# Values of the second layer made for 128 tokens and for four images' compressed rows at a time

## The reference, cut to what matters

```python
v = heads(x @ wv.T)                                      # values of the 64 tokens
windows = x[:, idx, :]                                   # 15 windows of 8 tokens
x_c = einsum('bwrd,r->bwd', windows, softmax(gate_logits))
k_c = x_c @ wk_c.T                                       # keys of the 15 compressed rows
v_c = x_c @ wv_c.T                                       # values of the 15 compressed rows
all_scores = concatenate([comp_scores, win_scores, sink], axis=-1)
attn = softmax(all_scores)
out = einsum('bhqk,bhkd->bhqd', w_comp, v_c) + einsum('bhqk,bhkd->bhqd', w_win, v)
```

## Time and profile before

| | us |
|---|---|
| median of three runs | 2063.84 |
| lowest and highest | 2058.97, 2075.73 |
| the profiled execution | 2071.78 |
| its span, first to last instruction | 2070.0 |

### The profile page before, as it was taken

One profiled execution on the slowest core, in us unless ns is written; L12 is line 12 of the kernel. 1 busy time (PEld: TensorE's weight loads), 2 busy tenths in 40 slices (PEclk: granted clock), 3 DMA queues, 4 the chain that ended last, 5 costly groups with the idle time before them and its releaser, 6 DMA issues.

```text
span 2070.0 us, 47437 instructions
## 1 busy us (share of the span) xinstructions
PE 1745.7 (84%) x15216; PEld 1352.3 (65%) x15216; DVE 1268.4 (61%) x3484; ACT 948.9 (46%) x2291; POOL 950.9 (46%) x770
## 2 busy tenths in 40 slices
PE   1454879989897989899897989899897989998956
PEld 1443766868676776768676776768675776866644
DVE  2566456757675766767575766767675756753432
ACT  0122534546463645456363635445463635553522
POOL 1224245454556555464456464464445554533222
PEclk9999988989999999999898989999998989999986
DMA  6647454544544444545445444544445444301000
GB/s 245 243 163 255 179 201 167 194 154 152 203 183 168 181 168 175 199 148 192 157 178 204 181 155 155 211 158 172 165 168 209 179 136 170 131 20 50 17 26 6
DMA packets 109170, 332.08 MB, mean 160 GB/s; under 512 B 13662, under 2 KB 87585, under 8 KB 92412
## 3 DMA queue, kind: packets, MB, share of 16 engines
q1 hardware_dynamic: 86416, 300.90, 39.5%
q0 software_dynamic: 8992, 19.42, 2.9%
q10 hardware_dynamic: 13516, 8.51, 1.4%
HBM read 299.48 MB, written 29.29 MB: 159 GB/s over the span
## 4 chain that ended last, share of the span: by engine, by line
PE 65%; POOL 10%; issue 9%; DMA 7%; DVE 4%; ACT 2%; ACTq 1%; SPq 1%; POOLq 0%; DVEq 0%
PE hid_bank L598 11%; PE pool_bank L452 6%; DMA outs_d<-ys 5%; PE pool_bank L457 5%; POOL yg L1357 5%; PE sec_bank L654 4%; PE hid_bank L583 4%; PE sec_bank L674 4%; PE hid_bank L582 3%; PE sec_bank L665 3%; POOL xbuf L1346 3%; PE hid_bank L584 2%; PE sec_bank L617 2%; PE sec_bank L634 2%; PE down_bank L543 2%
## 5 line engine op out<-in xcount | busy, mean ns | idle before, releaser
L1346 POOL TENSOR_TENSOR xbuf<-xbuf 128x512 f32<-128x512 f32 x256 | 330.1, 1289 | 528.3 <-DVE xbuf L1039 518.5
L850 ACT ACTIVATE hid<-hid_bank,bias_t 128x128 f32<-128x128 f32 x960 | 273.7, 371 | 122.3 <-PE hid_bank L584 116.4
L598 PE MATMUL hid_bank<-w_s,hid 128*128 x1920 | 291.3, 297 | 0.0
L598 PEld LDWEIGHTS hid_bank<-w_s,hid 128*128 128x128 f32 x1920 | 243.8, 199 | 16.7
L1039 DVE TENSOR_TENSOR xbuf<-xbuf 128x1536 f32<-128x1536 f32 x128 | 236.7, 1849 | 25.9 <-DMA xbuf<-in_x 25.9
L582 PE MATMUL hid_bank<-xt,w_b 128*128 128x128 bf16 x960 | 201.3, 230 | 33.8 <-issue 18.4
L1060 DVE SCALAR_TENSOR_TENSOR taps<-pooled_s,tapw,taps 128x256 f32<-128x256 f32 (+1 forms) x416 | 210.0, 505 | 29.9 <-issue 21.6
L1043 DVE TENSOR_TENSOR xbuf<-xbuf 128x512 bf16<-128x512 f32 x128 | 90.3, 706 | 213.5 <-ACT xbuf L764 213.4
L1384 POOL TENSOR_TENSOR keys_h<-keys,heads 128x632 f32<-128x632 f32 x128 | 198.6, 1578 | 18.1 <-PE sec_bank L654 15.6
L1200 DVE COPY ys<-hid_bank 128x128 f32<-128x128 f32 x240 | 68.8, 287 | 219.0 <-PE hid_bank L598 192.8
L583 PE MATMUL hid_bank<-xt,w_b 128*128 128x128 bf16 x960 | 202.9, 230 | 0.1
(11 more groups left out here) (213 smaller groups left out, 3443.7 us busy)
## 6 DMA issues: line engine op xcount, KB each, us to landing
xbuf<-in_x SPq DMA_DIRECT2D x128, 2048.0 KB
rows_s<-rows_d SPq DMA_DIRECT2D x48, 320.0 KB, 8.9
outs_d<-ys SPq DMA_DIRECT2D x240, 64.0 KB
out<-h ACTq DMA_DIRECT2D x16, 256.0 KB
w_s<-in_w ACTq DMA_DIRECT2D x1, 2560.0 KB
hid<-in_w POOLq DMA_DIRECT2D x10, 256.0 KB, 3.7
rows_d<-x2r,spot_i POOLq DMA_INDIRECT x128
yg<-outs_d,spot_i POOLq DMA_INDIRECT x128
```

The lines of the kernel that those rows point to most:

```text
L598: mm = nc.tensor.matmul(hid_bank[n % 2][:, 0:P], hid[:, n % RING, q * P:(q + 1) * P], w_q, start=False, stop=q == FC - 1)
L850: ins = nc.scalar.activation(hid[:, n % RING, cols], hid_bank[n % 2][:, cols], ACT.Gelu, bias=bias_t[:, q, j:j + 1])
L1346: nc.gpsimd.tensor_tensor(v[:, :, 1, :], v[:, :, 1, :], v[:, :, 2 * k + 3, :], ALU.add) \
```

## The change

`xc` gets 32 columns for each image in place of 15, and is cleared once in the set-up, so that four images' compressed rows are 128 columns. pre.6 makes the values of all tokens of the group, 128 tokens (two images) a product, four products. pre.7 makes the values of the compressed rows, four images a product, two products. ScalarE then moves the result from the partitions on which it came out to each image's: two moves of 64 partitions behind pre.6, four of 15 partitions behind pre.7, where there were two of 79 in all. The lists of all five engines are written anew.

```diff
     sp="""
-        store.9' load.0.0 store.11' load.0.1 store.12' store.10' store.13' store.14' rows.0 rows.1 load.1.0
-        load.1.1 load.2.0 store.0 store.3 load.2.1 store.1 rows.2 store.5 load.3.0 store.2 load.3.1 store.4
-        store.6 store.8 store.7 keep.0""",
+        store.8' store.4' store.6' store.7' load.0.0 store.9' store.12' store.11' store.10' load.0.1 store.13'
+        store.14' rows.0 load.1.0 load.1.1 rows.1 store.2 load.2.0 load.2.1 store.3 rows.2 store.1 store.0
+        store.5 load.3.0 load.3.1 keep.0""",
     pe="""
-        up.0 up.1 table up.2 down.0 up.3 down.1 up.4 up.5 down.2 out' up.6 down.3 down.4 pool.0.0 pool.0.1
-        pool.0.2 up.7 down.5 down.6 att.1 down.7 att.2 lift.0 pool.0.3 lift.1 widen.0 widen.1 lift.2 att.3
-        narrow.0 pre.2 narrow.1 lift.3 widen.2 att.4 pre.3 lift.4 narrow.2 lift.5 pool.1.0 pre.4 pool.1.1 widen.3
-        pre.5 pre.6 pre.7 widen.4 narrow.3 score.0 pool.1.2 score.1 pool.1.3 lift.6 att.7 score.2 score.3 widen.5
-        lift.7 score.4 score.5 narrow.4 score.6 score.7 att.8 widen.6 lift.8 narrow.5 turn.0 widen.7 turn.1
-        lift.9 value.0 pool.2.0 pool.2.1 narrow.6 turn.2 pool.2.2 widen.8 value.1 lift.10 pool.2.3 turn.3 lift.11
...
+        table up.0 up.1 up.2 down.0 up.3 down.1 up.4 down.2 down.3 up.5 out' down.4 pool.0.0 pool.0.1 down.5 up.6
+        pool.0.2 up.7 down.6 att.1 down.7 pool.0.3 lift.0 att.2 lift.1 widen.0 widen.1 att.3 lift.2 narrow.0
+        pre.2 widen.2 pre.3 lift.3 narrow.1 narrow.2 lift.4 pre.4 widen.3 pre.5 lift.5 pre.6 att.4 pool.1.0
+        pool.1.1 pre.7 lift.6 widen.4 narrow.3 score.0 score.1 lift.7 pool.1.2 widen.5 score.2 lift.8 score.3
+        pool.1.3 lift.9 score.4 score.5 narrow.4 att.7 score.6 score.7 lift.10 att.8 narrow.5 widen.6 turn.0
+        lift.11 widen.7 turn.1 value.0 pool.2.0 pool.2.1 narrow.6 turn.2 value.1 widen.8 turn.3 value.2 pool.2.2
...
     act="""
-        hidden.0 table hidden.1 hidden.2 hidden.3 hidden.4 inner.0.0 hidden.5 out' hidden.6 inner.0.1 hidden.7
...
-        inner.1.0 lift.4 gate pre.5 att.6 widen.3 pool.1.0 pre.6 pre.7 lift.5 inner.1.1 pool.1.2 lift.6 widen.4
-        widen.5 pool.1.3 att.7 lift.7 exp inner.2.0 lift.8 turn.0 widen.6 turn.1 pool.2.0 widen.7 inner.2.1
...
+        hidden.0 table hidden.1 hidden.2 hidden.3 inner.0.0 hidden.4 out' hidden.5 inner.0.1 pool.0.0 hidden.6
...
+        inner.1.0 pool.0.3 pre.5 widen.3 lift.5 pre.6 pool.1.0 pre.7 lift.6 widen.4 lift.7 inner.1.1 widen.5
+        lift.8 att.6 gate lift.9 att.7 pool.1.2 exp pool.1.3 lift.10 inner.2.0 turn.0 widen.6 turn.1 inner.2.1
...
-        xc = sb("xc", [C, GI, LC])
+        xc = sb("xc", [C, GI, 2 * LCP])
+        xcw = xc[:, :, 0:LC]
...
-                    half = n - 6
-                    bank = sec_bank[1 - half]
-                    eng.wait_ge(xc_step, at(xc_step, g, 8))
-                    if half == 0:
+                    if n == 6:
                         eng.wait_ge(rope_read, at(rope_read, g, 4))
+                        for t in range(T):
+                            mm = nc.tensor.matmul(b1[:, t * C:(t + 1) * C], x3t[:, t * P:(t + 1) * P], second["v"][:],
+                                                  start=True, stop=True)
                     else:
+                        eng.wait_ge(xc_step, at(xc_step, g, 8))
                         eng.wait_ge(kc_ready, at(kc_ready, g, 1))
-                    for m in range(4):
-                        im = 4 * half + m
-                        nc.tensor.matmul(bank[0:L, m * C:(m + 1) * C], x3t[:, im * L:(im + 1) * L], second["v"][:],
-                                         start=True, stop=True)
-                        mm = nc.tensor.matmul(bank[L:LK, m * C:(m + 1) * C], xc[:, im, :], second["vc"][:],
-                                              start=True, stop=True)
+                        for k in range(2):
+                            mm = nc.tensor.matmul(b0[:, k * C:(k + 1) * C],
+                                                  xc[:, 4 * k:4 * k + 4, :].rearrange("p i w -> p (i w)"), second["vc"][:],
+                                                  start=True, stop=True)
                     mm.then_inc(v_done, 1)
...
-                    half = n - 6
-                    eng.wait_ge(v_done, at(v_done, g, half + 1))
-                    nc.scalar.activation(values[0:LK, 4 * half:4 * half + 4, :, 0:HD].rearrange("p i h d -> p (i h) d"),
-                                         sec_bank[1 - half][0:LK, :].rearrange("p (m d) -> p m d", d=HD), ACT.Copy).then_inc(v_ready, 1)
+                    eng.wait_ge(v_done, at(v_done, g, n - 5))
+                    if n == 6:
+                        if after(g, 1):
+                            eng.wait_ge(o3_done, at(o3_done, g, 0))
+                        for im in range(2):
+                            ins = nc.scalar.activation(values[0:L, im:GI:2, :, 0:HD],
+                                                       b1[im * L:(im + 1) * L].rearrange("p (t h d) -> p t h d", t=T, d=HD),
+                                                       ACT.Copy)
+                    else:
...
+                        for im in range(4):
+                            ins = nc.scalar.activation(values[L:LK, im:GI:4, :, 0:HD],
+                                                       b0[im * 2 * LCP:im * 2 * LCP + LC, 0:2 * C]
+                                                       .rearrange("p (k h d) -> p k h d", k=2, d=HD), ACT.Copy)
+                    ins.then_inc(v_ready, 1)
...
+                nc.gpsimd.memset(xc[:], 0.0).then_inc(ready_p, 1)
                 nc.gpsimd.memset(values[:], 0.0).then_inc(ready_p, 1)
```

More of the change, by code:

```diff
@@ L35 @@
 LK = L + LC
+LCP = 16
 HH = HEADS // 2
@@ L67 @@
-        lift.9 value.0 pool.2.0 pool.2.1 narrow.6 turn.2 pool.2.2 widen.8 value.1 lift.10 pool.2.3 turn.3 lift.11
[L68 to L71, removed]
-    act="""
-        hidden.0 table hidden.1 hidden.2 hidden.3 hidden.4 inner.0.0 hidden.5 out' hidden.6 inner.0.1 hidden.7
-        att.1 pool.0.0 att.2 lift.0 pool.0.2 lift.1 widen.0 widen.1 lift.2 att.3 pre.2 lift.3 pool.0.3 widen.2
-        inner.1.0 lift.4 gate pre.5 att.6 widen.3 pool.1.0 pre.6 pre.7 lift.5 inner.1.1 pool.1.2 lift.6 widen.4
-        widen.5 pool.1.3 att.7 lift.7 exp inner.2.0 lift.8 turn.0 widen.6 turn.1 pool.2.0 widen.7 inner.2.1
[L77 to L80, removed]
@@ L81 @@
-    dve="""
[L82 to L90, removed]
+        table up.0 up.1 up.2 down.0 up.3 down.1 up.4 down.2 down.3 up.5 out' down.4 pool.0.0 pool.0.1 down.5 up.6
@@ new lines @@
+        narrow.7 pool.2.3 att.10 turn.4 lift.12 value.3 widen.9 turn.5 narrow.8 value.4 att.11 turn.6 value.5
+        narrow.9 widen.10 turn.7 value.6 widen.11 value.7 pool.3.0 narrow.10 lift.13 att.12 post.0 widen.12
+        post.1 pool.3.1 narrow.11 lift.14 pool.3.2 narrow.12 widen.13 widen.14 pool.3.3 narrow.13 narrow.14
+        post.3 post.4 post.5""",
+    act="""
+        hidden.0 table hidden.1 hidden.2 hidden.3 inner.0.0 hidden.4 out' hidden.5 inner.0.1 pool.0.0 hidden.6
+        hidden.7 att.1 pool.0.2 lift.0 lift.1 att.2 widen.0 widen.1 lift.2 att.3 pre.2 widen.2 lift.3 lift.4
+        inner.1.0 pool.0.3 pre.5 widen.3 lift.5 pre.6 pool.1.0 pre.7 lift.6 widen.4 lift.7 inner.1.1 widen.5
+        lift.8 att.6 gate lift.9 att.7 pool.1.2 exp pool.1.3 lift.10 inner.2.0 turn.0 widen.6 turn.1 inner.2.1
+        turn.2 widen.7 pool.2.0 turn.3 pool.2.2 high lift.11 turn.4 widen.8 att.10 lift.12 turn.5 pool.2.3
+        widen.9 inner.3.0 turn.6 turn.7 widen.10 pool.3.0 widen.11 lift.13 post.0 widen.12 inner.3.1 lift.14
+        pool.3.2 widen.13 widen.14 pool.3.3 post.3 post.4 post.5 weights.0 weights.1 weights.2 weights.3
+        weights.4 weights.5 weights.6 weights.7 weights.8 weights.9""",
@@ new lines @@
+    dve="""
+        tap.1.8' tap.1.9' pair.0.0 tap.1.10' tap.1.11' tap.1.12' tap.1.13' tap.1.14' inner.0.0 pair.0.1 att.0
+        inner.0.1 att.1 mix moe pre.1 pre.2 pair.1.0 narrow.0 pre.5 pre.3 narrow.1 pre.4 inner.1.0 narrow.2
+        pair.1.1 att.4 narrow.3 score.0 score.1 att.5 inner.1.1 score.2 score.3 score.4 score.5 pair.2.0 score.6
+        score.7 att.7 narrow.4 att.8 narrow.5 tap.0.0 tap.0.1 inner.2.0 pair.2.1 tap.0.2 value.0 att.9 tap.0.3
+        narrow.6 gate inner.2.1 value.1 tap.0.4 att.10 value.2 tap.0.5 tap.0.6 tap.0.7 narrow.7 tap.0.8 tap.0.9
+        tap.0.10 tap.0.11 rest value.3 pair.3.0 narrow.8 value.4 att.11 value.5 narrow.9 value.6 inner.3.0
+        pair.3.1 value.7 narrow.10 att.12 post.1 inner.3.1 narrow.11 post.2 narrow.12 tap.0.12 tap.0.13 low
+        post.3 narrow.13 narrow.14 tap.0.14 tap.1.0 tap.1.1 tap.1.2 tap.1.3 tap.1.4 tap.1.5 tap.1.6 post.5
+        tap.1.7 weights.0 weights.1 weights.2 weights.3 weights.4 weights.5 weights.6 weights.7 weights.8
+        weights.9""",
@@ L91 @@
     pool="""
[L92 to L95, removed]
+        gather.0 gather.1 gather.2 gather.3 gather.4 add.0.0 add.0.1 gather.5 gather.6 gather.7 add.0.2 add.0.3
@@ L96 @@
```

(9 more changed lines are left out.)

4 lines of the change are left out of this document (2 added, 2 removed).

## The result

The changed kernel takes 2116.12 us (median of 4 runs, 2111.44 to 2122.67); the kernel before took 2069.78 us beside it. The ratio is 1.0231, with a 95% interval of 1.0168 to 1.0294. The prediction was 2109 us, slower.

What follows compares the result with a forecast made beforehand. Taken as bound by TensorE's program order: 2071.78 − 63.7 (values) + 63.7 (lift.10's wait) + 4 (first iteration) + 35 (clock) + 6 (smaller loss) = 2116.8 us, by the median 2109. The 8-of-10 range was 2050 to 2145 us.

Steps and rivals of the forecast that it cites:

- The values: pre.6 and pre.7 on TensorE: six products take 1.50 us for 5.48, saving 3.98 us a group, 63.7 us over 16.
- lift.10's wait: TensorE waits at lift.10 for late rows.2: 4.9 us in 13 iterations, 63.7 us, plus 4 us in the first.
- The clock: Behind lift.10's gap TensorE's clock falls to half: 2.7 us in each of 13 iterations, 35 us.
- The smaller loss: At pool.0.0's gap, down.4 and up.6 come behind ScalarE's wait for GpSimd's additions: 1 us each time, 6 us in all.
- ScalarE: Moves of values take 1.55 us more a group, two table loads fewer expected; both costed at nothing.
- Rival 1: At lift.10 the values' gain arrives whole, rows.2 landing within 5.4 us of pool.1.3 or TensorE late anyway: 2000 us; 15%.
- Rival 2: The wait at lift.10 is there but the clock behind it stays up: 2064 to 2074 us by the median; 22%.
- Rival 3: store.9 lands late behind load.0.0, holding narrow.14's copy: 1 to 2 us in 14 iterations, 2123 to 2137 us; 10%.
- The sum: Whole run: savings and losses together give 2116.8 us, 2109 us by the median, slower by about 2%.

Runs made afterwards that it cites:

- e3: Kernel before (old products and moves) with the five new engine lists: 2185.4 us, ratio 1.0568.
- e1: Changed kernel with rows.2 issued ahead of load.2.1 in SyncE's list: 2060.5 us, ratio 0.9964.
- e15: Changed kernel with 19 unused products of 384 columns ahead of lift.10's wait, in all groups but the last two: 2120.88 us.
- e5: Changed kernel with 22 unused products of 384 columns ahead of lift.10's wait, in all groups but the last two: 2114.53 us.
- e13: Kernel before with the five new lists and rows.2 ahead of load.2.1: 2111.54 us, ratio 1.0179.
- e2: Changed kernel's new products, moves and xc with the five lists of the kernel before: 2150.39 us, ratio 1.0393.
- e7: Changed kernel with rows.2 ahead of load.2.1 and load.0.1 behind the stores store.13' and store.14': 1994.78 us, ratio 0.9627.
- e11: Kernel before with load.0.1 moved behind store.14' in SyncE's list: 2021.28 us, ratio 0.9769.
- e12: e7 with hidden.4 and hidden.6 ahead of the inner additions in ScalarE's list: 2010.13 us, ratio 0.9704.

## Why the prediction was right, point by point

- **The values.** Predicted 1.50 us for the six products, measured 1.47; 3.98 off, measured 4.01. A product with 128 columns of weights takes 1.47/6 = 0.25 us, one with 64 or 15 took 5.48/16 = 0.34: fewer columns made none of them cheaper. In the ledger the work at full clock falls by 3.0 only. The new lists alone raise it by 1.2 (e3 against before), which would account for the rest; no such term was in the sum.
- **lift.10's wait.** Predicted 13 × 4.9 = 63.7 and 4 in the first iteration; measured 57.0 in 14 waits, the longest 5.1, the first 4.7. The arrival 5.4 us after pool.1.3 was met. The landing at 10.3 was met in three iterations; in the others it came some 1.2 us sooner, so the usual wait was 3.6 to 4.0 us. The mechanism was right, the size 0.8 us an iteration too large. That the wait decides the result is shown by e1, in which it alone goes.
- **The clock.** Predicted 2.7 us an iteration; the ledger says 2.0, of which 1.9 lies right behind lift.10. The place and the cause hold: the clock falls there in eleven of eleven iterations with the gap and in none without it (e15, e5, e1, e13). The size was 0.7 too large. What does not follow is that closing the gap wins the time: with it filled (e15) or gone (e1) the loss of the whole iteration stays at 9.3 or 9.2, with long stretches at half clock in other places.
- **The smaller loss.** Its place was right: the gap of pool.0.0 became one ahead of down.4, 56.5 us in 17 waits. The idle time rose by 5.0, of which the wait is 57.0/14 = 4.1 and this and other small waits 0.9; I had 0.5.
- **ScalarE.** Costed at nothing. The table loads halved as expected (16 at L852 and 15 at L806, where three lines had 31, 16 and 16 before), and ScalarE's busy time fell from 948.9 to 930.4 us. The small moves take 375 ns each, and score.0 waits for them once in the run, 2.4 us at 2072 us, in the drain.
- **Rival 1, the gain whole,** failed on the landing: 7.6 us at the least, where it needed rows.2 within 5.4 us of pool.1.3. The Trainium skill ("DMA: Bandwidth & Descriptors", on two DMAs through the same engine) allows one transfer of a queue to end ahead of an earlier one; for rows.2 this trace does not show it: in all 14 iterations it landed 1.2 to 1.3 us behind load.2.1.
- **Rival 2, the clock stays up,** failed in the trace (0.50 behind the gap, in every steady iteration) and in the time.
- **Rival 3, a late store.9,** did not come about: VectorE's waits for a store's landing are 13.5 us in 9 over the run, against 9.9 before.
- **The sum.** In the steady iterations I had −4.0 + 4.9 + 2.7 + 0.5 = +4.1 us; measured +4.0. By kind: work −3.0 for −4.0, idle +5.0 for +5.4, low clock +2.0 for +2.7. The saving was put too high and so were both losses, and the errors cancelled; the direction rests on the wait, the closeness of the number is luck.

## What to carry to other kernels

Price a saving in the order in which it will stand: what a long instruction covered (here a chain over ScalarE and VectorE in e2) starts to show when it gets short. Then follow each queue of transfers past the place where its reader moves to: one 2 MB load ahead of a small transfer cost some 4 us an iteration at lift.10 (e1) and 5 in the stores of the expert rows (e7), and moving one issue by two places in a list gave 56 and 66 us, where the shorter products with all their lists were worth 26 once both orders were mended (e7 against e11). A gap of the busiest engine and the low clock behind it are two terms. Whether the gap is the cause is read iteration by iteration, with the gap and without it; whether closing it pays is read from the time of the whole run, for the clock can fall somewhere else.

## What was not expected of the hardware

- The granted clock fell to 0.50 for 37.5 us in which TensorE was busy throughout, right behind 32 us with 31.27 busy at clock 1.00 (e15). Such stretches of 20 to 41 us stand in one or two of the eleven steady iterations of e1, e5, e7, e12 and e15, all with the new values and lists and no long wait at lift.10, and in none of the other nine traces. It is not known from these runs what started them.
- In e2 a gap of 2.2 us went with 13.7 us at half clock from 836.8 us on, longer than the 10.2 and 4.1 us of work behind gaps of 5 us in the kernel before; products without use in its place took 40 us off the run, while at lift.10 they took off nothing.
